# Edge groups of 128 partitions by 8 in place of 125 by 8, in a four-layer graph network kernel

## What is computed

```python
# layer 0: weighted mean of the neighbours
agg = segment_sum(x[src] * edge_weight[:, None], dst, N)
out = x @ W_self.T + (agg / segment_sum(edge_weight, dst, N)[:, None]) @ W_neigh.T + bias   # then / norm(out)
# layer 1: sum of relu(neighbour + edge features)
h = x + segment_sum(relu(x[src] + edge_attr), dst, N)
out = relu(h @ W1 + b1) @ W2 + b2
# layer 2: linear messages, batch norm over the nodes, leaky relu
h = segment_sum(concat([x[dst], x[src] - x[dst]]) @ W.T + b, dst, N)
# layer 3: for each of 8 relations r, attention over the edges of type r (and a self loop per node)
h = x @ W[r];  e = leaky_relu((h @ a_src)[src] + (h @ a_dst)[dst])
alpha = softmax of e over the edges that share dst
out += segment_sum(alpha[:, None] * h[src], dst, N) + bias[r]
```

## Time and profile before

| | |
|---|---|
| device time, median of 3 runs | 12490.7 us (12488.14 to 12494.66) |
| span of the profiled execution, first to last instruction | 12467.0 us |
| POOL busy | 8333.5 us, 67% |
| PE busy / DVE busy / ACT busy | 3728.1 / 3306.4 / 333.1 us |

### The profile page before, as it was taken

The page is one execution under the profiler, slowest core; times in us unless marked ns, Lnnn a source line. Parts: engine busy times, 40 slices in busy tenths (PEclk is TensorE's granted clock), DMA queues, the critical chain, the costliest instruction groups (busy, mean ns, idle before and its releaser), DMA issues.

```text
span 12467.0 us, 100980 instructions
## 1 busy us (share of the span) xinstructions
PE 3728.1 (30%) x17532; PEld 3060.4 (25%) x17533; DVE 3306.4 (27%) x5890; ACT 333.1 (3%) x656; POOL 8333.5 (67%) x6852
## 2 busy tenths in 40 slices
PE   2223322342222222422222223650000000003558
PEld 2222222332222222322222222220000000003555
DVE  2222222241111111311111111322222222395554
ACT  0000000010000000000000000100000000000000
POOL 7777777648888888388888887037777777302443
PEclk6555555555555555555555555555555555556885
DMA  1111111111111111111111111132222222202220
GB/s 41 22 22 22 22 22 22 23 44 42 42 42 42 42 42 42 37 22 22 22 22 22 22 22 24 53 110 70 70 69 70 69 70 70 43 0 52 71 69 19
DMA packets 711832, 515.30 MB, mean 41 GB/s; under 512 B 532950, under 2 KB 558550, under 8 KB 711675
## 3 DMA queue, kind: packets, MB, share of 16 engines
q0 software_dynamic: 307200, 218.65, 9.5%
q1 hardware_dynamic: 378602, 238.73, 7.1%
q10 hardware_dynamic: 26000, 57.60, 1.6%
HBM read 403.71 MB, written 103.77 MB: 41 GB/s over the span
## 4 chain that ended last, share of the span: by engine, by line
POOL 57%; issue 20%; DVE 7%; PE 7%; DMA 5%; DVEq 2%; another core or an unknown queue 1%; ACT 0%; POOLq 0%; SPq 0%; ACTq 0%; PEldq 0%
POOL gat L494 57%; DMA idx<-key_d 2%; DVE oh L953 2%; DMA gat<-rel_d,idx 1%; PE p_a L785 1%; DVEq L221 1%; PE p_sum L842 1%; PE p_sum L819 1%; PE p_tr L693 1%; PE p_a L739 0%; PE p_sum L780 0%; PE p_b L836 0%; PE p_a L834 0%; DMA edge_w<-alpha_d 0%
## 5 line engine op out<-in xcount | busy, mean ns | idle before, releaser
L494 POOL DMA_INDIRECT gat<-x_d,idx x3200 | 4014.5, 1255 | 1316.6 <-issue 1316.6
L494 POOL DMA_INDIRECT gat<-rel_d,idx x1600 | 1944.5, 1215 | 1002.1 <-issue 985.9
L687 PE MATMUL p_sum<-oh,msg 125*66 125x128 f32 (+1 forms) x6400 | 1452.8, 421 | 3488.3 <-ACT msg L571 1807.8
L494 POOL DMA_INDIRECT gat<-in_x,idx x1600 | 1936.6, 1210 | 507.1 <-issue 506.8
L687 PEld LDWEIGHTS p_sum<-oh,msg 125*66 125x66 f32 (+1 forms) x6400 | 1305.5, 229 | 3635.1 <-DVE oh L939 3635.1
L687 PE MATMUL p_sum<-oh,gat 125*64 125x128 f32 x3200 | 727.0, 420 | 1770.0 <-DMA gat<-x_d,idx 1770.0
L687 PEld LDWEIGHTS p_sum<-oh,gat 125*64 125x64 f32 x3200 | 652.1, 226 | 1844.6 <-issue 1844.6
L945 DVE TENSOR_TENSOR sum_t<-sum_t,p_sum 64x128 f32 (+1 forms) x600 | 168.4, 281 | 3255.3 <-PE p_sum L687 3255.3
L939 DVE SCALAR_TENSOR_TENSOR oh<-dstf,fine_col,iota 125x512 f32<-125x512 f32 x1200 | 848.2, 748 | 438.4 <-issue 293.8
L801 PE MATMUL p_sum<-trip_s,oht 128*128 x2376 | 204.7, 237 | 2218.0 <-DVE oht L1202 2218.0
L514 POOL TENSOR_TENSOR msg<-gat,edge_w 125x512 f32<-125x512 f32 x200 | 208.9, 1044 | 853.2 <-DMA gat<-he_d 605.0
(11 more groups left out here) (241 smaller groups left out, 3283.6 us busy)
## 6 DMA issues: line engine op xcount, KB each, us to landing
he_d<-gat ACTq DMA_DIRECT2D x200, 281.2 KB
gat<-he_d SPq DMA_DIRECT2D x200, 281.2 KB
gat<-x_d,idx POOLq DMA_INDIRECT x3200, 2.9
ea<-in_edge_attr SPq DMA_DIRECT2D x200, 250.0 KB
drow<-dst_d SPq DMA_DIRECT2D x200, 250.0 KB, 4.8
rel_d<-sum_t SPq DMA_DIRECT2D x14, 2016.0 KB, 6.7
gat<-in_x,idx POOLq DMA_INDIRECT x1600, 2.9
gat<-rel_d,idx POOLq DMA_INDIRECT x1600, 3.0
```

Of the source, the lines that this page charges most:

```text
L494: nc.gpsimd.indirect_dma_start(out=gat[:, q, s, 0:width], out_offset=None, in_=table, in_offset=bass.IndirectOffsetOnAxis(ap=idx[:, q, s:s ...
L687: ins = nc.tensor.matmul(p_sum[0:width, 0, 0:W], lhs(q, s), oh[:, 0, s, :], start=(s == 0), stop=(s == S - 1))
```

## The change

`P` goes from 125 to 128. A group then has 1024 edges, 200,000 is no multiple of that, and `G` becomes 196 with the last group filled up: `EP` = 200,704 edges. The 704 added edges have source 0, weight 0, type 0 and destination `NP - 1` = 12,543, a row past the last node that the node buffers have anyway. The inputs are padded where they are laid out for the kernel. `T` becomes 1568, `SG` 98, `IT` 49. The one-hot row `oht` has then exactly `S * W` = 1024 columns, so the memset of its last 24 falls away.

```diff
-P, S = 125, 8
+P, S = 128, 8
 GE = P * S
-G = E // GE
+G = -(-E // GE)
+EP = G * GE
...
-T = E // P
-SG = 100
+T = EP // P
+SG = G // 2
...
-    dst16_d = dram("dst16_d", (E,), i16)
-    trip_d = dram("trip_d", (E * 3,))
-    alpha_d = dram("alpha_d", (E,))
+    dst16_d = dram("dst16_d", (EP,), i16)
+    trip_d = dram("trip_d", (EP * 3,))
+    alpha_d = dram("alpha_d", (EP,))
...
-                    at = dve.snap(within(first + k * (W // FW), (N - 1) // FW))
+                    at = dve.snap(within(first + k * (W // FW), (NP - 1) // FW))
...
-            ch(vec.memset(oht[:, GE:S * W], 0.0))
...
-                        vec.tensor_scalar(oht[:, 0:GE], drow[:, q % 2, :], node_col[:, bass.ds(w, 1)], None,
+                        vec.tensor_scalar(oht[:, :], drow[:, q % 2, :], node_col[:, bass.ds(w, 1)], None,
...
+    padded = lambda a, v=0: np.pad(a, [(0, EP - E)] + [(0, 0)] * (a.ndim - 1), constant_values=v)
     grouped = lambda a: a.reshape(G, P, S).transpose(1, 0, 2)
+    src, dst, kind = padded(i["src"]), padded(i["dst"], NP - 1), padded(i["edge_type_8"])
```

More of the change, by code:

```diff
@@ L225, in within @@
             return nc.s_assert_within(v, 0, most, skip_runtime_bounds_check_because=(
-                "a group's last window holds its largest dst, which is below N"))
+                "a group's last window holds its largest dst, which is below NP"))
         def out_of_order(eng):
@@ L974, in piped_pass @@
                 ch(vec.memset(sum_t[0:width, :], 0.0))
-                first_window(0, 0, within(group_windows(dve, 0, 0)[0], (N - 1) // FW))
+                first_window(0, 0, within(group_windows(dve, 0, 0)[0], (NP - 1) // FW))
                 with dve.Fori(0, IT) as it:
@@ L981, in piped_pass @@
                         following = group_windows(dve, 0, g + 1)
-                        first_window(1 - q % 2, g + 1, within(following[0], (N - 1) // FW))
+                        first_window(1 - q % 2, g + 1, within(following[0], (NP - 1) // FW))
                         wait_reg(dve, s_oh[4][1], it * Q + (q + 2))
-                        add(q % 2, within(first, (N - 1) // FW), cum + 1)
+                        add(q % 2, within(first, (NP - 1) // FW), cum + 1)
                         dve.sem_inc(s_more, 1)
@@ L1482 @@
     }
-    args = [given("x", i["x"]), given("src_p", grouped(i["src"])), given("dst_p", grouped(i["dst"])),
-            given("type_p", grouped(i["edge_type_8"])), given("weight_p", grouped(i["edge_weight"])),
-            given("dst_f", i["dst"]), given("type_f", i["edge_type_8"]), given("edge_attr", i["edge_attr_64"]),
+    args = [given("x", i["x"]), given("src_p", grouped(src)), given("dst_p", grouped(dst)),
+            given("type_p", grouped(kind)), given("weight_p", grouped(padded(i["edge_weight"]))),
+            given("dst_f", dst), given("type_f", kind), given("edge_attr", padded(i["edge_attr_64"])),
             {name: given(name, laid[name]) for name, _ in WEIGHTS}]
```

## The result

The changed kernel takes **12,571.97 us** (median of 5 runs, 12,552.54 to 12,626.76), the kernel before 12,490.7. The ratio is 1.0072, with a 95% interval of 1.0062 to 1.0083: slower by 0.7%, where 10,424 us and a gain of 17% were forecast. The profiled execution has a span of 12,570.2 us.

A forecast was written before the change was run, and what follows sets the result against it. POOL's back-to-back indirect gathers were taken as the bound. From 12,490.7 us, cheaper gathers (1756), fewer gathers (194), direct transfers (85) and small terms (16, 9, 7), 2067 together, gave 10,424 us; range 9,800 to 12,250.

The forecast's parts named there:

- dummies: In the old gather, five engines carry 25 rows each; the other eleven get 25 dummy elements of 4 bytes.
- both rivals on the list term: List length costs nothing, 12,180 us, chance 0.28; gather cost goes by real rows, about 12,362 us, chance 0.05.
- the list term: POOL's gathers: 17 fewer list entries at 16.5 ns save 0.28 us each, 1756 us over 6272 gathers.
- my reading of the earlier trace: A DVE instruction held up during a gather shows POOL writing its lists from 0.52 to 0.95 us.
- the stretch: At least 0.43 us of each gather in which POOL holds something DVE needs, taken as writing the lists.
- 0.43 / 26: Price of a list entry: 0.43 us over 25 entries and a closing one, 16.5 ns each.
- the transfers on the path: Trip and alpha stores and reloads behind pass 3: sixteen engines in place of five save 85 us.
- The sum: All terms together: 2067 us saved, from 12,490.7 to 10,424 us.
- so POOL stays the bound and nothing is late behind it: In the gather passes, eight gathers take 9.9 us, still above 6.5 us of DVE and PE work a group.
- the step on the cost of a gather: In the gather passes: a gather falls from 1.21 to 0.93 us on POOL, saving 1756 us.
- the fewer gathers: Each gather pass has 1568 in place of 1600, 128 fewer at 1.51 us: 194 us saved.
- DVE's collisions: Rival: DVE one-hots hit more gathers in the changed rhythm, +627 us, 12,807 us in all; chance 0.05.

The follow-up runs named there:

- before_120: Kernel before, each gather fetching 120 of its 125 rows, gather buffers cleared once first: 12,812.59 us, against 12,490.06 for the kernel before.
- narrow_rows: Changed kernel with rows of 64 bytes in place of 256 in pass 0 alone and one buffer memset first, on chip A: 10,512.71 us.
- half_rows: Changed kernel gathering 64 rows in place of 128 each time, buffers cleared first: 12,659.53 us.
- memset_first: Changed kernel plus one VectorE memset of the gather's buffers ahead of everything, full rows: 12,645.26 us.
- narrow_again: The kernel of narrow_rows run again on another chip, beside the unaltered changed kernel: 12,701.13 us, against 12,647.80 for the changed kernel.
- before_posts: Kernel before with 1, 2 and 4 extra 16-row transfers a group on SyncE's queue in passes 0, 1, 2: 12,468.62 us.
- before_incs: Kernel before with 16, 32 and 64 semaphore increments a group by SyncE itself in passes 0, 1, 2: 12,468.48 us.
- pace_16: Changed kernel with a POOL memset of 16 columns behind every gather, each waited for: 11,848.88 us.
- pace_16_timed: The kernel of pace_16 timed in more runs: 11,877.53 us, ratio 0.9511 to the kernel before.
- pace_rare: The kernel of pace_16 with its semaphore cleared once for 32 gathers in place of 8: 11,818.66 us, ratio 0.9461 to the kernel before.
- pace_loops: Changed kernel with empty POOL loops: one turn behind each gather in passes 0 and 3, 8 turns behind each group in pass 1: 12,326.92 us.

## Why the prediction was wrong

**Right, the gather.** 1568 a pass; 32 packets each on queue 0, and only the 64 surplus bytes of 16 closing writes (no dummies); the direct store has 28,224 / 196 = 144 packets. The gather fell from 1.209 to 0.944 to 0.947 us, 0.26 where 0.28 was forecast: 15.6 ns an entry where I had 16.5. So both rivals on the list term are out. The dummies are borne out by before_120: 203.37 MB are some 96 bytes a gather over its rows, 16 closing writes and 8 dummies for its one idle engine. Of my reading of the earlier trace rows one half holds. In narrow_rows the one-hot of pass 3 can be seen against its gather:

```profile
8387.06 0.94 POOL L487 DMA_INDIRECT gat<-rel_d,idx  x1 [0.30 <-issue]
8387.53 0.72 DVE L1196 TENSOR_SCALAR oht<-drow,node_col 128x1024 bf16<-128x1024 int16 x1 [4.22 <-remote]
```

It ends 1.19 us behind the gather's start, so by its free 0.486 us it got going 0.71 behind it, against 0.95 in the kernel before; in half_rows, with lists of 4, it is 0.64. The end of the hold moves with the list's length: 0.24 us for 17 entries, 0.065 for 4. But the stretch is not the lists alone, as the forecast took it to be. In the changed kernel's runs it goes from 0.46 us (the one-hot is free when it starts at 0.45, held up at 0.47) to 0.71, 0.25 us where nine entries of 16.5 ns would be 0.15, and in half_rows it is 0.18 us for five. So a part of it does not go by this price, and that 0.43 / 26 came within 1 ns of the measured price was in part luck. The Trainium skill's page "DMA: Bandwidth & Descriptors" (section on the anatomy of a GpSimd DMA) calls this cost small. The measurement decides: with 17 entries fewer on its longest list a gather cost 22% less.

**Right, the transfers on the path.** The chain of narrow_rows behind pass 3 (start us, us, what), against 71.52, 20.49, 7.72 and 31.40 in the earlier trace rows:

```profile
8876.82 23.61 DMA trip_d<-trip
8900.45 8.59 DMA trip_s<-trip_d
...
9363.80 3.28 DMA alpha_d<-sum_t
9368.46 16.69 DMA edge_w<-alpha_d
```

52.2 in place of 131.1 us, -79 where -85 was forecast; only the last was mis-sized (9.8 forecast). The changed kernel has nearly the same landings (23.6, 8.5, 3.3, 16.6). The first gather starts at 11.36 us, forecast at about 10.

**The sum, where no signal is late.** In narrow_rows the passes take 8001 us, 1845 less than before (-1950 forecast; 6272 x 0.016 = 100 us of the difference is the list term), and all outside them 2510, -111 against the forecast -117. So 10,424 was off by 89 us for that execution. (The 9690 us in the forecast are 6400 x 1.514 and not x 1.51; no term hangs on it.)

**Wrong: "so POOL stays the bound and nothing is late behind it".** This sentence closes the step on the cost of a gather, and it is the step that failed. I compared DVE's and PE's work on a group, 6.5 us, with eight gathers, 9.9, and took the hand-over between engines as fixed at what the earlier trace rows shows. It is not. From the changed kernel to narrow_rows the passes differ by 10,009 - 8001 = 2008 us and the rest by 51, together the whole 2059 between the spans. The list term and the fewer gathers were earned by POOL and given back in waits for signals: POOL goes on back to back until its buffers are used up, and then stands still until a late signal has freed one. In the changed kernel 168 of the 337 late signals arrive while it stands, mostly some 4 us behind its last gather, the others while it still gathers. The nine executions with late signals and a period of 1.21 to 1.29 us all come out at 1.56 to 1.61 us a gather, whatever the gather itself takes (0.90 to 0.98); why at this value, no run shows. That it is so near the 1.54 us of the kernel before makes the result look like "no change"; nothing shows that this nearness is more than chance. No rival of mine had this; the one on the slower side, DVE's collisions, is out as well, since 6059.3 us for 6272 gathers are 0.966 each, 19 ns over the median where it was 25 before.

**Shown, and open.** Shown, on the chips that have it: the shorter gather, with its rows on more engines, is enough (before_120); the change's other parts, the start, row sizes and bytes are not needed (memset_first, narrow_again, half_rows), and increments by SP or on its queue are not enough (before_posts, before_incs); slowing POOL to 1.48 us a gather or more takes nearly all of it away (pace_16, pace_16_timed, pace_rare).

The long register instructions go with the late signals through all runs: 1182 to 1316 over 0.5 us in each of the eight executions with over 100 late groups a pass and no loops, 2485 in pace_loops with its many more, 22 to 157 in the three with a few late groups, at most 11 in all others.

Not shown: whether the pace as such helps or that POOL does something else between gathers, since all pauses that made the period longer are memsets, and a loop that did not still helped a little; what it is that holds signals and instructions back; and what chip A, or that execution, has that the others have not.

One observation goes with it: the trace of the changed kernel holds 48,970 records of semaphore changes where that of narrow_rows holds 148,326 for nearly the same work. So records are lost where signals are late. But pace_16_timed, with a single late group, has only 106,499, so records can be lost with hardly a late signal. The Trainium skill's page "NOTIFIC — the notification-queue block" (section 7.1 on overflow) says that a full record queue drops new records, overwrites old ones or stalls the engine that makes them. Loss, lateness and register instructions of 0.70 us would fit that, but every execution timed here was also recorded, so no run shows whether the late signals exist without the recording.

## What to carry to other kernels

When one engine issues back to back and you make its step cheaper, the time of the hand-over to the others is part of the forecast: price not only their work but how soon their signals come, and give the case in which the freed time returns as waits a real chance. Read it from what ends the waits: the same wait that was ended by "PE p_sum" and is now ended by "remote", with the matmul long done, is a late signal and not a slow matmul. Look then at the instructions that only compute in registers as well: if some of them take many times their median, it is more than one signal. Where it shows, a small pause on the fast engine can be worth more than its cost (here 5.4% under the kernel before), and a result from one chip should be seen on a second before it is believed.

## What the runs showed of the hardware

- A matmul's signal reached VectorE up to 30 us late (8 us or more in the median of most passes' late groups) while GpSimd issued an indirect gather every 1.21 to 1.29 us; at 1.51 us it never was late. Of the lettered chips five ran a kernel at such a pace, and on one of them, in its one such execution, no signal was late: 10,512.7 us there and 12,701.1 on another, for the same kernel.
- In the executions with over 100 late groups a pass about 4% of the register-only instructions (6.5% in pace_loops), on VectorE and SyncE above all, took over 0.5 us, mostly 0.70 us, in place of some 0.03 to 0.12; on GpSimd too where it had a loop (pace_loops). None did in the kernel before.
- An indirect gather cost POOL by the entries of its longest engine list: 1.209 us with 25, 0.944 with 8, 0.903 with 4, so 15.6 ns an entry between the first two and 10 between the last. With 15 engines of 8 rows (before_120) it was 0.982, 38 ns above that of 16 engines; I don't know why.
- On POOL, behind a memset, a wait for a computed semaphore value costs 0.81 us before the next gather, one for a constant 0.27; between two gathers nothing of it shows beside the usual 0.30.
